# Preparing the mixture's first expert and four tiles inside the cross attention, widening four tiles at a time, and counting the first stage's loads apart

## The chip, the cores and the metric

The kernel runs on one core of a Trainium2 chip. The core has five engines that matter here, each with its own queue of instructions, carried out in order: TensorE (PE in the profile, PEld for its weight loads), VectorE (DVE), ScalarE (ACT), GpSimd (POOL) and SyncE (SP), which here only issues transfers between HBM and the on-chip memory SBUF. Matmuls write into eight PSUM banks of 128 partitions by 512 fp32 values. Engines wait for each other through counting semaphores. The metric is the time of the whole program on the device in microseconds (us), the median of three runs.

## The reference

Two decoder layers over 32 sequences of 64 rows with 256 features, so 2048 rows, 16 tiles of 128 rows. Each of the six sublayers takes a layer norm of x and adds its result to x:

```python
x = x + _L0_attn_ref(_layernorm(x), ...)                      # differential attention with rotary, causal
x = x + _L0_xattn_ref(_layernorm(x), ctx_2048, ctx_2048, W)   # attention over features
x = x + _L0_ffn_ref(_layernorm(x), ...)
x = x + _L1_attn_ref(_layernorm(x), ...)                      # state space
x = x + _L1_xattn_ref(_layernorm(x), ctx_2048, mask, ...)     # grouped cross attention, 16 heads of 128
x = x + _L1_ffn_ref(_layernorm(x), ...)                       # mixture of 8 experts
```

The mixture is what most of the change is about (Wg, Wu, Wd are 8 x 256 x 256):

```python
weights = _router_weights(x, Wr, temperature)
gate = jnp.einsum('btd,edf->ebtf', x, Wg)
up = jnp.einsum('btd,edf->ebtf', x, Wu)
...
mid = jax.nn.silu(gate) * up
out = jnp.einsum('ebtf,efd->ebtd', mid, Wd)
...
return jnp.einsum('bte,ebtd->btd', weights, out)
```

Two of the eight experts have a low-rank addition to each matrix.

## The kernel before

The six sublayers follow one another; at each end all semaphores are cleared and all engines meet at a barrier (`end_sublayer`, L59 to L63). x stays in SBUF throughout. A layer norm (`RowNorm`) has three parts: small DVE steps on the row statistics (`on_vector`), two ACT steps (`on_scalar`), and one DVE operation for each tile (`normalise`, L119). `keep_clock` (L74 to L77) issues matmuls of the identity whose result nobody reads; each shows as two PE rows of the trace.

**Stage one, `differential_attention`.** A hand-written software pipeline: `turn(t)` for t from -3 to 16, in which tile t+3 is normalised, turned (a transpose through PE) and projected, tile t+2 is rotated by the rotary tables, tile t+1 is scored and tile t is mixed. The order of each engine is the order in which `turn` is written. SP loads x in four parts of 512 KB, the identity, the projections and seven constants; the seven share one semaphore, `loaded`, with LOADS = 7 * 16. At the end of its turn -3 DVE runs `lambda_dots`, which waits for all seven; DVE's next steps are the second tile's normalisation and the first rotation. PE waits for the same semaphore, and for `wo_scaled`, before it projects the second tile.

**The cross attention, `grouped_attention`.** Again turns; LAST is 15, the turn of the last tile, and turn 16 mixes that tile, multiplies it with the output weights (L2386, L2390) and adds it to x (L2266). The sublayer owns three large buffers shared with the one before: `raw` (called `staged` by the caller), `w_q_high` and `w_q_low`. The last queries read the two halves of w_q in turn 14.

**Split operands.** For fp32 accuracy at the speed of the fp32r type a number is kept as a high part (an ACT or DVE cast) and a low part (the number less its high part). `three_passes` (L1919 to L1923) is three matmuls: high by high, low by high, high by low. Every large matmul of the cross attention and of the mixture goes through L1923 or is written out in the same way.

**The mixture, `mixture`.** x is taken as PAIRS = 8 pairs of tiles, and there are STEPS = 64 steps, step s being expert s // 8 and pair s % 8. On PE a step is widen(s), then a few small jobs in the first steps (turn_x, route_x, fold), then narrow(s - 2):

- widen(s): for each half f of the 256 middle features, gate and up, each over two chunks of 128 inputs in three passes. That is 12 matmuls of 256 columns for each f, 24 in a step. The results of one f lie in one bank, gate in its first half and up in its second.
- then ACT takes silu of the gate (L2589), DVE multiplies with up (`middle`, L2723), ACT casts the product to its high part (`middle_high`, L2576), DVE subtracts to get the low part (`middle_low`, L2728).
- narrow(s): 12 matmuls of 256 columns with the down matrix. It waits until both low parts of step s are there. DVE adds the result to x, weighted by the router (`add`, L2748; for expert one also `add_held`, L2734).

Before the first widening the mixture loads expert 2's three matrices (M_ORDER starts with 2), casts and subtracts them, and normalises, turns and splits the first pair. PE fills this time with `keep_clock`.

## Time and profile before

| | us |
|---|---|
| three runs, median (lowest to highest) | 1317.61 (1316.46 to 1317.67) |
| the profiled execution, its own time | 1319.73 |
| its span, first to last instruction | 1317.8 |
| PE busy | 1205.5 (91% of the span) |
| DVE busy | 961.0 (73%) |
| ACT busy | 707.0 (54%) |
| POOL busy | 464.9 (35%) |
| mean granted PE clock | 0.974 of full speed |

Full speed of the PE clock is 2.4 GHz, and it is granted in two levels, 2.4 and 1.2 GHz; in a window row the clock is a mean over the window. A bracket at the end of a timeline row gives how long the engine sat idle before it and what released it. The duration of a matmul row reaches to its modelled end, past the start of the next one, so PE's pace is read from the distance of starts.

### The profile page before, as it was taken

What the parts mean: (1) busy time and instruction counts of PE and PEld (TensorE: products, weight loads), DVE (VectorE), ACT (ScalarE), POOL (GpSimd) and SP (SyncE); (2) the same over time, 40 slices, a digit from 0 to 9 for tenths busy, and PEclk for the clock granted to TensorE, in tenths of its full rate; (3) what the DMA queues carried; (4) which work ended last, traced back from release to release, by engine and by line L of the source; (5) the groups of instructions that cost most, each with busy time, mean ns of one, the idle gap of its engine ahead of it and who ended that gap; (6) DMA issues with size and microseconds to landing.
All of it is one profiled execution on the core that took longest, in us unless ns stands there. A gap on an engine that the chain in (4) does not pass through costs nothing. (4 is left out here: it accounts for less than half of the span.)

```text
span 1317.8 us, 27466 instructions
## 1 busy us (share of the span) xinstructions
PE 1205.5 (91%) x9944; PEld 958.4 (73%) x9944; DVE 961.0 (73%) x1862; ACT 707.0 (54%) x1459; POOL 464.9 (35%) x553
## 2 busy tenths in 40 slices
PE   4999997988888778898899999999997999999998
PEld 3677764444443657797678878787886999999998
DVE  5889986899996467786668777786775768555555
ACT  2778863788888355001565665656562563333332
POOL 1444642456563134565552324233230301112210
PEclk8999997899999879899999999999999999999999
DMA  5111161133331300001200000000000300000001
GB/s 174 37 36 37 43 150 34 42 81 96 90 88 30 114 1 0 1 0 65 85 9 4 8 4 4 8 4 8 4 1 11 87 25 25 25 25 25 1 1 65
DMA packets 60709, 51.05 MB, mean 39 GB/s; under 512 B 9064, under 2 KB 52936, under 8 KB 60232
## 3 DMA queue, kind: packets, MB, share of 16 engines
q1 hardware_dynamic: 60622, 49.88, 13.6%
q8 instruction: 56, 0.92, 0.3%
q14 instruction: 31, 0.25, 0.1%
HBM read 37.93 MB, written 11.53 MB: 38 GB/s over the span
## 5 line engine op out<-in xcount | busy, mean ns | idle before, releaser
L208 DVE TENSOR_REDUCE stacks_neg_max<-psum 128x2 f32<-128x512 f32 x256 | 164.0, 686 | 29.1 <-PE psum L204 28.1
L947 ACT ACTIVATE fa_probs<-psum 128x1024 f32<-128x1024 f32 x128 | 130.7, 1023 | 36.0 <-PE psum L1072 36.0
L1923 PE MATMUL psum<-mo_xT_high,mo_w_high 128*128 128x256 f32 x512 | 144.5, 282 | 1.7 <-DVE mo_xT_low L2757 1.6
L1923 PE MATMUL psum<-mo_xT_low,mo_w_high 128*128 128x256 f32 x512 | 144.2, 282 | 0.0
L1923 PE MATMUL psum<-mo_xT_high,mo_w_low 128*128 128x256 f32 x512 | 143.5, 280 | 0.0
L2589 ACT ACTIVATE mo_silu<-psum 128x256 f32<-128x256 f32 x128 | 49.0, 384 | 155.0 <-PE psum L1923 155.0
L2723 DVE TENSOR_TENSOR mo_mid<-mo_silu,psum 128x256 f32<-128x256 f32 x128 | 53.6, 420 | 92.8 <-ACT mo_silu L2589 92.7
L2059 POOL TENSOR_TENSOR ga_probs<-ga_probs,ga_top 128x1024 f32<-128x1024 f32 x16 | 30.5, 1904 | 203.7 <-DVE ga_top L2213 203.7
L204 PE MATMUL psum<-stacks_k_stack,stacks_q_stack 48*128 48x256 bf16 x512 | 89.8, 283 | 9.9 <-DVE stacks_neg_max L208 6.5
L1923 PEld LDWEIGHTS psum<-mo_xT_high,mo_w_high 128*128 128x128 f32 x512 | 96.3, 188 | 2.2 <-DVE mo_xT_low L2757 1.7
L1923 PEld LDWEIGHTS psum<-mo_xT_low,mo_w_high 128*128 128x128 f32 x512 | 96.4, 188 | 0.0
L1923 PEld LDWEIGHTS psum<-mo_xT_high,mo_w_low 128*128 128x128 f32 x512 | 96.3, 188 | 0.0
L2530 POOL TENSOR_TENSOR mo_w_low<-mo_raw,mo_w_high 128x512 fp32r<-128x512 f32 x21 | 27.6, 1314 | 188.0 <-ACT mo_w_high L2564 188.0
L1072 PE MATMUL psum<-stacks_q_stack,stacks_k_stack 51*128 51x256 bf16 x512 | 86.8, 280 | 0.0
L2048 POOL TENSOR_TENSOR ga_q_scaled<-ga_q,ga_q_inv 128x1024 f32<-128x1024 f32 x32 | 70.1, 2191 | 38.0 <-ACT ga_q_inv L2090 38.0
L204 PEld LDWEIGHTS psum<-stacks_k_stack,stacks_q_stack 48*128 48x128 bf16 x512 | 32.7, 96 | 64.2 <-DVE stacks_neg_max L208 36.4
L2083 ACT ACTIVATE ga_q_scaled<-ga_q 128x512 f32<-128x512 f32 x64 | 40.2, 632 | 61.8 <-DVE ga_q L2186 61.8
L1923 PE MATMUL psum<-mo_w_high,mo_mid_high 128*128 128x256 f32 x256 | 72.3, 282 | 0.0
L1923 PE MATMUL psum<-mo_w_low,mo_mid_high 128*128 128x256 f32 x256 | 71.9, 281 | 0.0
L1923 PE MATMUL psum<-mo_w_high,mo_mid_low 128*128 128x256 f32 x256 | 71.7, 280 | 0.0
L1084 PE MATMUL psum<-fa_probs,fa_values 128*32 128x256 f32 x1024 | 70.3, 393 | 0.8 <-ACT fa_probs L947 0.6
L2386 PE MATMUL psum<-ga_w_o_high,ga_mixedT_high 128*128 128x256 f32 x256 | 64.2, 291 | 4.9 <-DVE ga_mixedT_low L2205 4.9
(432 smaller groups left out, 3548.3 us busy)
## 6 DMA issues: line engine op xcount, KB each, us to landing
k_parts<-da_k_parts SPq DMA_DIRECT2D x96, 64.0 KB, 2.0
stacks_k_stack<-k_parts SPq DMA_DIRECT2D x32, 192.0 KB
q_parts<-stacks_parts SPq DMA_DIRECT2D x48, 64.0 KB, 2.0
stacks_q_stack<-q_parts SPq DMA_DIRECT2D x32, 96.0 KB
x<-in_x SPq DMA_DIRECT2D x4, 512.0 KB, 7.7
da_context<-in_ctx SPq DMA_DIRECT2D x4, 512.0 KB, 7.3
stacks_q_stack<-q_parts SPq DMA_DIRECT2D x32, 64.0 KB
fa_context<-in_ctxT SPq DMA_DIRECT2D x16, 128.0 KB, 2.3
```

The costliest lines, as they stand in the source:

```text
L204: return core.nc.tensor.matmul(core.psum[:, bank, q * E:(q + 1) * E], self.q_stack[lane, slot, b, h // LANES, q * P:(q + 1) * P], self.k_s ...
L208: return core.nc.vector.tensor_reduce(self.neg_max[:, b, :, head_at(h)], core.psum[:, bank, :].rearrange("p (q k) -> p q k", q=2), AX.X, A ...
L947: nc.scalar.activation(probs[:, g].rearrange("p h k q -> p h (k q)"), ps[:, 2 + 2 * (g % 2):4 + 2 * (g % 2), :], ACT.Exp).then_inc(exp_don ...
L1072: return nc.tensor.matmul(ps[:, 2 + h % 4, k * E:(k + 1) * E], k_stack[lane, slot, b, h // LANES, k * P:(k + 1) * P], q_stack[lane, slot, ...
L1084: done = nc.tensor.matmul(ps[32 * c:32 * c + 32, 6, half * E:(half + 1) * E], values[:, slot, k, 8 * b + head_at(h), :], probs[:, h // 2, ...
L1923: done = nc.tensor.matmul(out, lhsT[i], rhs[j], start=start and k == 0, stop=stop and k == 2)
L2048: nc.gpsimd.tensor_tensor(q_scaled[:, columns].rearrange("p (h d) -> p h d", d=G_HD), q[:, columns].rearrange("p (h d) -> p h d", d=G_HD), ...
L2059: nc.gpsimd.tensor_tensor(probs[:], probs[:], top[:, :, None].to_broadcast([P, G_HEADS, SEQ]), ALU.subtract).then_inc(shifted, 1)
L2083: nc.scalar.activation(q_scaled[:, g * G_CHUNK:(g + 1) * G_CHUNK], q[:, g * G_CHUNK:(g + 1) * G_CHUNK], ACT.Square).then_inc(squares_ready, 1)
L2386: nc.tensor.matmul(ps[:, 6, 0:E], mixedT_high[:, h], weight[:, h], start=(h == 0 and weight is w_o_high), stop=False)
L2589: nc.scalar.activation(silu[:, j % 4], ps[:, j % 4, 0:2 * P], ACT.Silu).then_inc(silu_ready, 1)
L2723: nc.vector.tensor_tensor(mid[:, j % 4], silu[:, j % 4], ps[:, j % 4, 2 * P:4 * P], ALU.mult).then_inc(mid_ready, 1)
```

## The change

It has three parts.

1. In stage one the loads are reordered and counted in three groups: `rotary_loaded` (rotary tables and head mask), `causal_loaded`, and `loaded` with three loads left. The identity comes first, x in part 1 comes behind the rotary tables, parts 2 and 3 later still. `lambda_dots` moves from DVE's turn -3 to its turn -2. PE runs `keep_clock(core, 6, 12)` before the pipeline and `keep_clock(core, 6, 8)` in turn -1.
2. The cross attention's last two turns prepare the mixture. SP loads the first expert's matrices into `staged`; in turn 15 ACT casts them and POOL subtracts them (into the space of w_q_high and w_q_low), and DVE normalises eight tiles with a layer norm of its own for these (`lead_ln`); in turn 16 PE turns the first four tiles, ACT copies them, DVE casts them and POOL subtracts them. The mixture uses these buffers in place of its own and starts with widen(0).
3. The mixture widens four tiles at once: widen(s) is now one half f for two pairs, 12 matmuls of 512 columns, gate in one bank and up in another. silu, middle, middle_high and middle_low run once a step on 512 columns in place of twice on 256. narrow(s) waits for the low parts of both steps of its four tiles, and the last four narrowings follow the last widening.

```diff
@@ differential_attention
+        loaded, rotary_loaded, causal_loaded = sem("loaded"), sem("rotary_loaded"), sem("causal_loaded")
-        LOADS = 7 * 16
+        LOADS = 3 * 16
...
+            first_rows.load_ident(sp)
             first_rows.load(sp, 0)
-            first_rows.load_ident(sp)
-            for out, src in ((w_qk[:], chunked(dram["da_w_qk"])), (w_v[:], chunked(dram["da_w_v"]))):
+            for out, src in ((w_v[:], chunked(dram["da_w_v"])), (w_qk[:], chunked(dram["da_w_qk"]))):
                 sp.dma_start(out, src).then_inc(projection_loaded, 16)
-            for g in range(1, first_rows.PARTS):
-                first_rows.load(sp, g)
-            for out, src in ((rotary[:], dram["rotary"]),
-                             (head_mask[:], dram["da_head_mask"]), (causal[:], dram["causal"]), (causal_rows[:], dram["causal_rows"]),
-                             (lam_in[:], dram["da_lam"]), (w_o[:], chunked(dram["da_w_o"])), (gain[:], dram["da_gain"]),
-                             ):
+            for out, src in ((rotary[:], dram["rotary"]), (head_mask[:], dram["da_head_mask"])):
+                sp.dma_start(out, src).then_inc(rotary_loaded, 16)
+            first_rows.load(sp, 1)
+            for out, src in ((causal[:], dram["causal"]), (causal_rows[:], dram["causal_rows"])):
+                sp.dma_start(out, src).then_inc(causal_loaded, 16)
+            first_rows.load(sp, 2)
+            for out, src in ((lam_in[:], dram["da_lam"]), (w_o[:], chunked(dram["da_w_o"])), (gain[:], dram["da_gain"])):
                 sp.dma_start(out, src).then_inc(loaded, 16)
+            first_rows.load(sp, 3)
...
@@ vector engine
+                    if at(t, -2):
+                        dve.wait_ge(rotary_loaded, 32)
...
-                if isinstance(t, int) and t == -3:
+                if isinstance(t, int) and t == -2:
                     lambda_dots()
...
@@ tensor engine
+                    if at(t, -1):
+                        pe.wait_ge(causal_loaded, 32)
+                    if at(t, 0):
+                        pe.wait_ge(wo_scaled, KC)
...
+                if at(t, -1):
+                    keep_clock(core, 6, 8)
...
-                    if at(t, -2):
-                        pe.wait_ge(loaded, LOADS)
-                        pe.wait_ge(wo_scaled, KC)
...
+            keep_clock(core, 6, 12)
             pipeline(pe, turn)
@@ grouped_attention, sync
+            for k, name in enumerate(("gate", "up", "down")):
+                sp.dma_start(ahead.raw[:, k], chunked(dram[f"mo_w_{name}"][M_ORDER[0]])).then_inc(ahead_loaded, 16)
...
@@ gpsimd engine
+                if isinstance(t, int) and t == LAST:
+                    for k in range(M_MATRICES):
+                        pool.wait_ge(ahead_w_highs, k + 1)
+                        nc.gpsimd.tensor_tensor(ahead.w_low[:, k], ahead.raw[:, k], ahead.w_high[:, k].bitcast(F32), ALU.subtract).then_inc(ahead_w_lows, 1)
+                if isinstance(t, int) and t == TILES:
+                    for n in range(ahead.PAIRS):
...
+                        nc.gpsimd.tensor_tensor(ahead.pair(ahead.xT_low, n), ahead.xT[:, n], ahead.pair(ahead.xT_high, n).bitcast(F32),
...
@@ scalar engine
+                if isinstance(t, int) and t == LAST:
+                    act.wait_ge(ahead_loaded, 16 * M_MATRICES)
+                    act.wait_ge(q_psum, 4 * TILES)
+                    for k in range(M_MATRICES):
+                        nc.scalar.copy(ahead.w_high[:, k], ahead.raw[:, k]).then_inc(ahead_w_highs, 1)
+                if isinstance(t, int) and t == TILES:
+                    for n in range(ahead.PAIRS):
+                        act.wait_ge(ahead_xT_psum, n + 1)
+                        nc.scalar.copy(ahead.xT[:, n].rearrange("p c t -> p (c t)"), ps[:, 2 + n, :]).then_inc(ahead_xT_ready, 1)
...
@@ vector engine
+                if isinstance(t, int) and t == LAST:
+                    dve.wait_ge(lead_ln.ready, 1)
...
+                    for n in range(ahead.TILES):
+                        lead_ln.normalise(ahead.xn[:, n // 2, n % 2], n).then_inc(ahead_xn, 1)
+                if isinstance(t, int) and t == TILES:
+                    for n in range(ahead.PAIRS):
...
+                        nc.vector.tensor_copy(ahead.pair(ahead.xT_high, n), ps[:, 2 + n, :].rearrange("p (c t) -> p c t", c=KC)).then_inc(ahead_x_highs, 1)
...
@@ tensor engine
-                        keep_clock(core, 2, 8)
+                        keep_clock(core, 2, 4)
                     pe.wait_ge(v_lows, t)
+                    if isinstance(t, int) and t == TILES:
+                        for n in range(ahead.PAIRS):
+                            turn_ahead(n)
@@ mixture, scalar
-                for f in range(FT):
-                    j = FT * s + f
-                    act.wait_ge(wide_psum, j + 1)
-                    nc.scalar.activation(silu[:, j % 4], ps[:, j % 4, 0:2 * P], ACT.Silu).then_inc(silu_ready, 1)
-                    if j >= 1:
-                        middle_high(j - 1)
+                act.wait_ge(wide_psum, s + 1)
+                nc.scalar.activation(silu[:, s % 2], ps[:, s % 2 * 2 + GATE, :], ACT.Silu).then_inc(silu_ready, 1)
+                middle_high(s)
...
@@ vector engine
-                if s >= PAIRS + LAG + 1:
+                if PAIRS + LAG + 1 <= s < STEPS - 1:
                     add(s - LAG - 1)
...
+                middle(s)
+                middle_low(s)
...
@@ tensor engine
             def widen(s):
+                e, q, f = s // PAIRS, s % PAIRS // 2, s % 2
+                for k in (GATE, UP):
+                    for c in range(KC):
+                        columns = slice(f * P, (f + 1) * P)
+                        done = three_passes(nc, ps[:, s % 2 * 2 + k, :],
+                                            (w_high[e % RING][:, k, c, columns], w_low[e % RING][:, k, c, columns]),
+                                            (xT_high[q][:, c], xT_low[q][:, c]), start=(c == 0), stop=(c == KC - 1))
+                done.then_inc(wide_psum, 1)
...
+                pe.wait_ge(mid_ready, s - 1)
+                widen(s)
...
-                pe.wait_ge(mid_lows, FT * (s + 1))
+                pe.wait_ge(mid_lows, s // 2 * 2 + 2)
...
-            keep_clock(core, 2, 5)
-            turn_x(0)
-            keep_clock(core, 2, 4)
+            pe.sem_inc(xT_psum, ahead.PAIRS)
...
-                if s >= LAG:
+                if LAG <= s < STEPS - 2:
                     narrow(s - LAG)
-            for s in range(STEPS - LAG, STEPS):
+            for s in range(STEPS - LAG - 2, STEPS):
                 narrow(s)
```

DVE in stage one, from the first tile's normalisation (da_xn) on. Before:

```order
L119 TENSOR_SCALAR da_xn<-x,da_lead_mean,da_lead_rstd 128x256
L148 BN_STATS row_stats<-x 128x6 x4
L517 TENSOR_TENSOR da_lam_prod<-da_lam_in 128x16
L519 TENSOR_REDUCE da_lam_dot<-da_lam_prod 128x2
L521 TENSOR_SCALAR da_w_o<-da_w_o,da_gain 128x256 x2
L119 TENSOR_SCALAR da_xn<-x,da_lead_mean,da_lead_rstd 128x256
L559 TENSOR_TENSOR da_rot_b<-psum,da_rotary 128x384
```

And DVE after the change, in the same place:

```order
L119 TENSOR_SCALAR da_xn<-x,da_lead_mean,da_lead_rstd 128x256
L148 BN_STATS row_stats<-x 128x6 x4
L119 TENSOR_SCALAR da_xn<-x,da_lead_mean,da_lead_rstd 128x256
L567 TENSOR_TENSOR da_rot_b<-psum,da_rotary 128x384
L568 TENSOR_TENSOR da_rot_a<-psum,da_rotary 128x384
L574 STREAM_SHUFFLE da_rot_c<-da_rot_b 128x384
L590 TENSOR_TENSOR da_rot<-da_rot_a,da_rot_c 128x384
L148 BN_STATS row_stats<-x 128x6 x4
L523 TENSOR_TENSOR da_lam_prod<-da_lam_in 128x16
```

The lambda steps have moved behind the second tile's normalisation, its rotation and the third part's statistics.

PE from the end of the cross attention into the mixture, before (the two branches stand at the barrier, mo_xn are the normalised rows of the first pair):

```order
L2390 MATMUL psum<-ga_w_o_high,ga_mixedT_low 128x256 x16
L77 MATMUL psum<-ident 128x128 x4
L1938 UNCONDITIONAL_BRANCH
L2784 UNCONDITIONAL_BRANCH
L77 MATMUL psum<-ident 128x128 x5
L2793 MATMUL psum<-ident,mo_xn 128x128 x4
L77 MATMUL psum<-ident 128x128 x4
L1923 MATMUL psum<-mo_xT_high,mo_w_high 128x256
```

And PE after the change; here w_q_high and w_q_low hold the first expert and the first four tiles:

```order
L2455 MATMUL psum<-ga_w_o_high,ga_mixedT_low 128x256 x16
L77 MATMUL psum<-ident 128x128 x4
L1950 UNCONDITIONAL_BRANCH
L2851 UNCONDITIONAL_BRANCH
L1935 MATMUL psum<-w_q_high 128x512
L1935 MATMUL psum<-w_q_high,w_q_low 128x512
L1935 MATMUL psum<-w_q_low,w_q_high 128x512
```

Nothing stands between the barrier and the first widening, and that has 512 columns.

DVE in the cross attention's turn 15 and the start of turn 16, after the change (staged is where the eight normalised tiles go; before, the row with x8 at L119 and the row at L2314 are not there):

```order
L2304 TENSOR_TENSOR ga_probs<-ga_probs,ga_inv 128x1024
L119 TENSOR_SCALAR staged<-x,ga_lead_mean,ga_lead_rstd 128x256 x8
L2317 TENSOR_TENSOR x<-x,psum 128x256
L2326 TENSOR_TENSOR ga_probsT_low<-psum,ga_probsT_high 128x1024
L2330 BN_STATS row_stats<-x 128x6
L2246 SCALAR_TENSOR_TENSOR ga_mixedT_low<-psum,ga_bias_v,ga_mixedT_high 128x4x64 x8
L2314 CAST w_q_high<-psum 128x2x256 x2
```

The eight normalisations stand ahead of tile 14's addition to x, and the two casts ahead of tile 15's.

## Rows read from the trace of the kernel before

**Rows 1.** The chain that ended last: start us, us, what, in the mixture.

```profile
1066.74 246.87 PE psum L1923 x2088
```

**Rows 2.** Timeline, stage one: start us, us, engine, line, operation, [idle before <-releaser].

```profile
10.00 1.41 DVE L148 BATCH_NORM_STATS2 row_stats<-x 128x6 f32<-128x256 f32 x4 [1.69 <-DMA x<-in_x]
...
15.48 0.18 DVE L517 TENSOR_TENSOR da_lam_prod<-da_lam_in 128x16 f32<-128x16 f32 x1 [4.08 <-DMA da_gain<-in_da_gain]
...
16.30 0.41 DVE L119 TENSOR_SCALAR da_xn<-x,da_lead_mean,da_lead_rstd 128x256 f32<-128x256 f32 x1
...
18.93 2.77 PE L762 MATMUL psum<-da_xT,da_w_qk 128*128 128x128 f32 x12
18.96 1.90 POOL L408 TENSOR_TENSOR da_keys<-da_rot,da_head_mask 128x1024 f32<-128x1024 f32 x1 [16.54 <-DVE da_rot L582]
...
21.63 0.61 PE L653 MATMUL psum<-da_causal,da_causal_rows 64*128 64x512 bf16 x2
...
23.69 1.23 DVE L537 TENSOR_REDUCE da_top<-psum 128x16 f32<-128x1024 f32 x1 [0.86 <-PE psum L657]
...
28.81 1.50 PE L762 MATMUL psum<-da_xT,da_w_qk 128*128 128x128 f32 x12
```

**Rows 3.** Windows: stretch, length, busy time by engine, granted clock, DMA share, GB/s.

```profile
4.00:8.00 4.00, 0.00 (x0) 0.00 (x0) 2.23 (x13) 0.50 (x2) 0.00 (x0) 1.00 0.99 338
16.00:20.00 4.00, 2.77 (x12) 2.37 (x12) 3.90 (x12) 1.27 (x6) 1.04 (x1) 0.50 0.84 261
```

**Rows 4.** Timeline, the cross attention's last two turns, columns as in rows 2.

```profile
999.70 1.23 DVE L2263 TENSOR_TENSOR ga_probs<-ga_probs,ga_inv 128x1024 f32<-128x1024 f32 x1
...
1004.28 1.01 ACT L2169 CAST ga_probsT_high<-psum 128x1024 fp32r<-128x1024 f32 x1 [6.69 <-PE psum L2415]
...
1016.67 0.42 DVE L2266 TENSOR_TENSOR x<-x,psum 128x256 f32<-128x256 f32 x1 [4.48 <-PE psum L2390]
```

**Rows 5.** Timeline, the mixture's start, PE and ACT, then DVE and POOL behind.

```profile
1018.90 1.35 PE L77 MATMUL psum<-ident 128*128 128x128 f32 x10 [1.38 <-PEq L62]
...
1021.60 0.62 ACT L2564 CAST mo_w_high<-mo_raw 128x512 fp32r<-128x512 f32 x1 [1.20 <-DMA mo_raw<-in_mo_w_gate]
...
1024.33 0.39 PE L1923 MATMUL psum<-mo_xT_high,mo_w_high 128*128 128x256 f32 x1 [1.55 <-DVE mo_xT_low L2757]
...
1026.04 1.38 DVE L119 TENSOR_SCALAR mo_xn<-x,mo_mean,mo_rstd 128x256 f32<-128x256 f32 x4
...
1031.62 2.57 POOL L2518 TENSOR_TENSOR mo_xT_low<-mo_xT,mo_xT_high 128x512 fp32r<-128x512 f32 x2 [0.96 <-DVE mo_xT_high L2630]
...
1032.06 2.93 DVE L119 TENSOR_SCALAR mo_xn<-x,mo_mean,mo_rstd 128x256 f32<-128x256 f32 x4
```

**Rows 6.** Timeline, PE's pace: 512 columns in the cross attention, 256 in the mixture.

```profile
856.34 0.39 PE L1923 MATMUL psum<-w_q_high,ga_xT_low 128*128 128x512 f32 x1
...
857.26 0.39 PE L1923 MATMUL psum<-w_q_low,ga_xT_high 128*128 128x512 f32 x1
...
857.69 0.69 DVE L2186 TENSOR_TENSOR ga_q<-psum,ga_bias_q 128x512 f32<-128x512 f32 x1 [0.55 <-PE psum L1923]
...
873.06 0.41 PE L1923 MATMUL psum<-ga_w_k_high,ga_ctxT_low 128*128 128x512 f32 x1
...
874.00 0.39 PE L1923 MATMUL psum<-ga_w_k_low,ga_ctxT_high 128*128 128x512 f32 x1
...
1102.19 0.28 PE L1923 MATMUL psum<-mo_xT_high,mo_w_high 128*128 128x256 f32 x1
...
1105.04 0.28 PE L1923 MATMUL psum<-mo_w_high,mo_mid_high 128*128 128x256 f32 x1
```

**Rows 7.** Timeline, mixture: a steady step's first two links, and a loaded step's DVE.

```profile
1089.31 1.92 DVE L2734 SCALAR_TENSOR_TENSOR x<-mo_held,mo_zone,x 128x256 f32<-128x256 f32 x2
...
1197.39 0.38 ACT L2589 ACTIVATE mo_silu<-psum 128x256 f32<-128x256 f32 x1 [1.64 <-PE psum L1923]
...
1197.80 0.42 DVE L2723 TENSOR_TENSOR mo_mid<-mo_silu,psum 128x256 f32<-128x256 f32 x1 [0.96 <-ACT mo_silu L2589]
```

219 lines of the change are left out of this document (115 added, 104 removed).

## The prediction, made before the changed kernel ran

> **What bounds the kernel now.** I read the chain of waits first, to see which engine ends last at each of the three places of the change, then the timelines there. In the mixture the chain stays on PE: its last piece is 2088 matmuls in 246.87 us, 0.1182 us each [rows 1]. So there PE's pace is the bound, and ACT, DVE and POOL cost nothing as long as they deliver in time. Between the barrier and 1024.33 it is not PE's pace that decides: PE issues clock-keeping matmuls from 1018.90 and waits for the first split operands [rows 5]. In stage one DVE is what the others follow: it idles 4.08 us for the seventh small load (da_gain), and at 16.30 makes the rows on which PE's second projection rests [rows 2]. The last turns of the cross attention are gaps on every engine but PE [rows 4].
>
> **Stage one.** DVE's order today: statistics of x's part 1 at 10.00 for 1.41, then the wait to 15.48, then the second normalisation at 16.30 [rows 2]. Afterwards no lambda wait stands between the two. Part 1 of x, however, now comes behind the rotary tables (384 KB). At 338 GB/s [rows 3] that is 1.15 us, so it lands near 11.1 in place of 10.0; the statistics end near 12.5 and the second normalisation starts there: 3.8 us earlier. The identity now goes ahead of x's part 0, one more issue of 0.5 us, which delays only the first tile and ends before DVE needs it.
>
> PE follows. Twelve rows of the projection take 2.77 us at 18.93, but 1.50 at 28.81 [rows 2]. The granted clock of 16 to 20 is 0.50 [rows 3], the level of 1.2 GHz; 1.50 is what the level of 2.4 GHz gives. PE had done nothing before its first turn, and idled before 16.77. The change fills the time from the identity's landing (near 3) to the first turn with 12 clock-keeping matmuls. I take it that the clock is then at its upper level for the second turn. Then the second tile goes so: normalised 12.9, turned 13.4, copied 14.0, projected with v (0.6) and q, k (1.5) by 16.3. The first keys come after rot_b, rot_a, shuffle and sum (together 2.2 us) and POOL's 1.90 [rows 2]: 12.9 + 2.2 + 1.9 = 17.0. The first scores start at 17.2 in place of 21.63 and take about 0.3 less, so the first maximum starts near 19.0 in place of 23.69 [rows 2]. DVE itself is free by then: rotation to 15.1, statistics of part 2 to 16.5, lambda steps 0.8 to 17.3, normalisation and two rotations to 18.7. From 23.69 on nothing changes in order but 8 clock-keeping matmuls, 16 PE rows or 2.0 us, where PE waits 2 us for DVE anyway. The gain is 4.6 us. If the clock stays at 1.2 GHz, PE decides: the second projection ends near 19.0 and the gain is 2.2. With part 1 landing as early as before it is at most 5.4.
>
> **The cross attention's last turns.** All that is added must fit into gaps; I price it engine by engine. ACT: three casts of 128x512 at 0.62 [rows 5] lie in its gap of 6.69 before 1004.28 [rows 4], two copies of 0.58 behind the last mixed heads. POOL: three subtractions of 128x512, 1.3 each [rows 5], between about 998.3 and 1002.5, and two in turn 16 that end near 1015.5, 2 us ahead of DVE's last operation; it has nothing else there. PE: 4 clock-keeping matmuls give way to 8 transposes, 8 rows for 8 rows. SP: three transfers, with nothing queued behind them but waits. DVE: eight normalisations start when the probabilities are done at 1000.93 [rows 4]. Four take 1.38 us alone, but 2.93 beside POOL's two subtractions [rows 5]: about 0.8 us extra for each subtraction overlapped. Here some 1.5 us of POOL are overlapped, so they take 2.8 + 1.0 = 3.8 and end near 1004.9. Queued behind them are tile 14's addition (0.42, as at 1016.67) and the low part of the probabilities, which cannot start before ACT ends at 1005.29 [rows 4]. That leaves 0.1 us of loss; with all eight slowed they take 5.9, and the loss would be 2.1. The two casts in turn 16 lie in DVE's gap of 4.48 before 1016.67 [rows 4].
>
> **The mixture's start.** PE could start at 1018.90, the first thing it does after the barrier, and starts real work at 1024.33 [rows 5]. Gain 5.4 us. What is late next? widen(0) and widen(1) need nothing more. widen(2) needs the second four tiles: their transposes follow widen(0) and end at 1018.9 + 2.8 + 1.0 = 1022.7; copies, casts and two subtractions of 1.3 bring them to about 1026.5, and PE comes to widen(2) at 1029.7. The four transposes of pair 1 are gone from PE's path too, 0.5 us at the pace of the keeping rows (ten in 1.35) [rows 5]. Together 5.9 us (5.4 to 5.9).
>
> **The widening.** 1536 matmuls of 256 columns become 768 of 512. From 1102.19 to 1105.04 are 24 starts, 0.1187 each, 0.2375 for two. In the cross attention four distances of 512-column matmuls take 0.92 us at 856.34 and 0.94 us at 873.06, so 0.230 and 0.235 each [rows 6]. The difference to 0.2375, times 768, is 5.8 us by the one and 1.9 by the other, and these are the bounds. Neither place is nearer to the mixture than the other, so I take the middle, 0.2325: 768 x 0.005 = 3.8 us.
>
> The Trainium skill, page TensorE: Matmul & The Clock Gate, section Back-to-back issue gap, puts the isolated gap at N/2.4 + 2.5 ns. By it, an estimate, two short matmuls cost 2.5 ns more than one long one and the 768 pairs save 1.9 us, the lower bound again. The 256-column rows lie 12 ns above N/2.4, so the trace doesn't agree with the fixed part.
>
> **The new wait.** narrow(s) for even s now waits for the low parts of widen(s+1). Between the end of widen(s+1) and that narrow PE has narrow(s-1) (12 x 0.118 = 1.4) and widen(s+2) (12 x 0.2325 = 2.8): 4.2 us of cover, where there were 8.5. The chain it must cover: hand-over from PE 0.2 (DVE starts at 857.69, 0.43 after the last 512-column start) [rows 6], silu 0.62, product 0.69, cast 0.62, subtraction 0.69 [rows 5, 6], three hand-overs of 0.03 [rows 7]: 2.9, say 3.0. It holds in steady steps. Two places are tighter. In the last steps narrow(62) has only narrow(60) and narrow(61) as cover, 2.8 us: a loss of 0.2. In the second expert's steps DVE has add_held beside POOL's subtraction, 1.92 us for two [rows 7] where two additions like that at 1016.67 would take 0.84 [rows 4]; three such steps in a row push the products back by about 1.1 us each, against 1.2 us of slack, which I follow through the queue to a loss of 0.4. Together 0.6 (0.2 to 3).
>
> **The sum.** 4.6 - 0.1 + 5.9 + 3.8 - 0.6 = 13.6 us. The profiled execution would come out at 1319.73 - 13.6 = 1306.1; it lies 2.1 above the median of the runs, so the forecast for the median is 1317.6 - 13.6 = 1304.0.
>
> **Rivals.**
> - The clock does not hold in stage one. For: PE's work there has gaps, and the trace shows the fall after such a gap. Against: the gaps are shorter now. Gain 2.2 in place of 4.6, so 1306.4.
> - The long matmuls keep a pace of 0.235 [rows 6]: 1.9 less 3.8 is 1.9 us lost, 1305.9.
> - The preparation is late or in the way: the eight normalisations hold back turn 15 by 2.1 us in place of 0.1: 1306.0. For: DVE and POOL slow each other [rows 5]. Against: only 1.5 us of POOL's work is left by then.
> - By the Trainium skill (the same page, Part 4: PE-mode transpose) a transpose does not keep the clock up as a matmul does. As a mechanism here: PE's eight clock-keeping rows give way to transposes at 1005, the clock falls to 1.2 GHz, and the 48 output matmuls run slower until it rises. Priced from the projection's 2.77 against 1.50 us for twelve rows, a stretch of 3 us at the lower level loses 1.4 us, so 1305.4, or twice that, 1306.8, if it lasts into widen(0). Against it: 8 matmul rows and all of the mixing stand beside the transposes in the same stretch.
> - Slower: the cover of 4.2 us does not hold in steady steps. The place is narrow(s) for 31 even s; the price is what the chain has above 4.2. It turns the change slower when 31 times the excess passes 13.6 us, that is from 0.44 us, a chain of 4.64. At 5.0 the excess is 0.8, and 31 x 0.8 = 25 us less 13.6 gives 1329. Against: the sum of rows is 3.0, and it needs a slowdown of ACT or DVE that no steady row shows.
> - The change doesn't do what it says, because the barrier and not the preparation sets the mixture's start: then 5.4 shrinks to 1 or 2, giving 1308. Against: clock-keeping matmuls start at 1018.90 already.
>
> **Chances.** Forecast 0.50; clock in stage one 0.20; pace 0.10; preparation late or transposes 0.13; steady waits slower 0.03; barrier 0.04. The range reaches from all upper bounds at once, 5.4 + 5.9 + 5.8 less 0.3, that is 1317.6 - 16.8 = 1300.8 and a little more, to two rivals together with the new wait at its bound, 1310: 1299.5 to 1309.5. About 0.2% or 2.6 us is what a measurement can tell from no change. All cases but the steady waits lie more than 7 us below: faster 0.95, same 0.02, slower 0.03.
>
> **What would show it.** The first widening row right behind the barrier, where the clock-keeping row stands today; no PE gap of over 0.5 us in the mixture but near steps 12 to 14 and narrow(62); starts of 512-column matmuls 0.2325 apart; the first maximum of stage one near 19.0 and its projection of the second tile in 1.5 us. A PE idle row ended by mo_mid_low in every second step would make the forecast wrong, as would a lambda or x wait of DVE past 13 us in stage one, or a cross-attention turn 15 longer than before.

## The result, and the profile after

The changed kernel takes 1305.56 us, the median of five runs (1303.46 to 1310.16); the kernel before takes 1317.61 (1316.46 to 1318.76) beside it. The ratio is 0.9914, with a 95% interval of 0.9898 to 0.9931, that is 9.1 to 13.4 us. Measured once more, the distance of the medians was 13.5 us (1305.40 against 1318.95, ratio 0.9914, 0.9891 to 0.9936). The forecast was 1304.0 with a range of 1299.5 to 1309.5. The ratios leave out one execution of the kernel before that took 2291.62 us.

The profiled execution of after took 1305.56 us, 14.2 less than that of before. Its page begins:

```profile
span 1303.5 us, 25721 instructions
PE 1201.9 (92%) x9190; PEld 920.7 (71%) x9190; DVE 946.5 (73%) x1737; ACT 697.7 (54%) x1333; POOL 470.2 (36%) x557
```

PE's busy time falls by only 3.6 us (1205.5 to 1201.9); the rest of the 14 us was waiting. These are the three places of the change.

**Stage one.** Timeline of after, DVE, PE and ACT (start us, us, engine, line, operation, [idle before <-releaser]); the rows answer to [rows 2]:

```profile
9.93 1.41 DVE L148 BATCH_NORM_STATS2 row_stats<-x 128x6 f32<-128x256 f32 x4 [0.81 <-DMA x<-in_x]
11.38 0.41 DVE L119 TENSOR_SCALAR da_xn<-x,da_lead_mean,da_lead_rstd 128x256 f32<-128x256 f32 x1
12.96 0.56 DVE L567 TENSOR_TENSOR da_rot_b<-psum,da_rotary 128x384 f32<-128x384 f32 x1 [1.18 <-PE psum L773]
...
19.15 1.21 DVE L543 TENSOR_REDUCE da_top<-psum 128x16 f32<-128x1024 f32 x1
```

```profile
10.63 2.23 PE L773 MATMUL psum<-da_xT,da_w_qk 128*128 128x128 f32 x12
...
14.70 1.50 PE L773 MATMUL psum<-da_xT,da_w_qk 128*128 128x128 f32 x12
...
17.32 0.39 PE L661 MATMUL psum<-da_causal,da_causal_rows 64*128 64x512 bf16 x2 [1.12 <-POOL da_keys L414]
```

The lambda wait is gone and the first maximum starts at 19.15 in place of 23.69, 4.54 us earlier. The second normalisation comes at 11.38, 4.9 us earlier. But DVE then waits 1.18 us for the first tile's projection, and the granted clock shows why. Windows of after (stretch, length, busy time by engine, granted clock, DMA share, GB/s):

```profile
8.00:11.00 3.00, 1.41 (x11) 1.12 (x11) 1.48 (x6) 1.05 (x4) 0.00 (x0) 1.00 1.12 343
11.00:14.00 3.00, 2.54 (x14) 2.14 (x13) 1.78 (x7) 1.24 (x5) 0.00 (x0) 0.53 1.11 336
14.00:17.00 3.00, 2.20 (x16) 2.01 (x16) 2.86 (x7) 1.04 (x4) 1.68 (x1) 0.90 1.09 385
```

The fall to 1.2 GHz has not gone. It stands at 11 to 14, on the first projection; the second, which lay in it before ([rows 3], 2.77), now runs in 1.50. The first was slow before as well, which neither the rows above nor the granted clock told. Timeline of before, PE:

```profile
10.59 2.44 PE L762 MATMUL psum<-da_xT,da_w_qk 128*128 128x128 f32 x12
```

The first maximum isn't the end of the stage. From it to the moment when PE passes the barrier behind stage one are 191.42 us before and 192.32 after, so of the 4.54 us 3.64 are left there (215.11 against 211.47). The prediction had put nothing for this loss of 0.9. The two sequences of maxima part by 0.28 at the fourth maximum and by 0.9 at the twentieth.

**The cross attention's last turns.** Timeline of after, PE, DVE and ACT; then the same two PE rows of before:

```profile
990.29 0.39 PE L2451 MATMUL psum<-ga_w_o_high,ga_mixedT_high 128*128 128x256 f32 x1 [2.53 <-DVE ga_mixedT_low L2246]
...
995.85 3.63 DVE L119 TENSOR_SCALAR staged<-x,ga_lead_mean,ga_lead_rstd 128x256 f32<-128x256 f32 x8
998.67 1.01 ACT L2210 CAST ga_probsT_high<-psum 128x1024 fp32r<-128x1024 f32 x1 [5.38 <-PE psum L2480]
999.73 1.21 DVE L2326 TENSOR_TENSOR ga_probsT_low<-psum,ga_probsT_high 128x1024 fp32r<-128x1024 f32 x1
1001.00 0.39 PE L2365 MATMUL psum<-ga_probsT_high,ga_values_high 64*128 64x256 f32 x2 [0.60 <-DVE ga_probsT_low L2326]
```

```profile
996.15 0.58 PE L2386 MATMUL psum<-ga_w_o_high,ga_mixedT_high 128*128 128x256 f32 x1 [2.53 <-DVE ga_mixedT_low L2205]
...
1006.65 0.38 PE L2303 MATMUL psum<-ga_probsT_high,ga_values_high 64*128 64x256 f32 x2 [0.62 <-issue]
```

From the first output matmul to the first mixing matmul it is 10.71 us now and was 10.50, but 10.77 in a second profile of before. DVE begins the low part at 999.73, 0.05 after ACT has ended (998.67 + 1.01 = 999.68). So two things end together here, and one profile can't say which is the limit; no_keep, below, can.

**The mixture's start.** Timeline of after; the row answers to those at 1018.90 and 1024.33 in [rows 5]:

```profile
1013.46 0.47 PE L1935 MATMUL psum<-w_q_high 128*128 128x512 f32 x1 [1.60 <-PEq L62]
```

The mixture's chain begins at 1013.27 and widening starts 0.19 later; before it was 1018.79 and 5.54. That is 5.35 us.

**The steps.** I count a step from the start of one widening to the next. Steps 0 to 9 take 55.74 us after (1013.46 to 1069.20) and 56.60 before; steps 10 to 61 take 218.65 after (1069.20 to 1287.85) and 221.17 before. From there to the end it is 15.7 in both. The chain of waits of after, in the mixture (start us, us, what), shows the one long interruption:

```profile
1054.77 1.63 PE psum L1935 x12
1056.39 0.02 issue
1056.42 0.59 ACT mo_held L2659
1057.00 0.02 issue
1057.02 1.28 ACT L2691
...
1062.72 0.70 DVE mo_mid_low L2804
1063.42 0.04 issue
1063.46 230.14 PE psum L1935 x1308
```

ACT loads its table for the router's exponentials (1.28), DVE's router steps follow, and the middle values of step 7 queue behind them. PE waits only 0.23 us for it: widening 8 takes 3.03 from its start to the next narrowing in place of 2.80.

In the pair of profiles, then, read from barrier to barrier: stage one 3.64; the second sublayer 0.72 and the third 0.30, which the change doesn't touch; the cross attention 0.94, in spite of 1.4 won in its first turn, which the change doesn't touch either; the mixture 8.66, of which 5.35 are its start, 0.86 steps 0 to 9 and 2.52 steps 10 to 61. That is 14.2 us, of which some 2 lie where no gain was forecast.

### The profile page after: what moved, and what is told of

The parts are those of the page before. It is cut to its first block and busy times, and to the rows that moved or that the text cites. A ratio compares the mean times of both kernels' runs of the same rounds, so it can differ in the third digit from the quotient of the medians.

```text
span 1303.5 us, 25721 instructions
## 1 busy us (share of the span) xinstructions
PE 1201.9 (92%) x9190; PEld 920.7 (71%) x9190; DVE 946.5 (73%) x1737; ACT 697.7 (54%) x1333; POOL 470.2 (36%) x557
## 5 line engine op out<-in xcount | busy, mean ns | idle before, releaser
L2672 ACT ACTIVATE mo_silu<-psum 128x512 f32<-128x512 f32 x64 | 38.3, 598 | 113.2 <-PE psum L1935 113.1
L2800 DVE TENSOR_TENSOR mo_mid<-mo_silu,psum 128x512 f32<-128x512 f32 x64 | 43.9, 685 | 73.0 <-ACT mo_silu L2672 72.9
L2804 DVE TENSOR_TENSOR mo_mid_low<-mo_mid,mo_mid_high 128x512 fp32r<-128x512 f32 x64 | 44.9, 702 | 44.0 <-ACT mo_mid_high L2663 44.0
L2663 ACT CAST mo_mid_high<-mo_mid 128x512 fp32r<-128x512 f32 x64 | 39.7, 620 | 56.4 <-DVE mo_mid L2800 56.4
L2451 PE MATMUL psum<-ga_w_o_low,ga_mixedT_high 128*128 128x256 f32 x256 | 62.9, 286 | 0.0
L2246 DVE SCALAR_TENSOR_TENSOR ga_mixedT_low<-psum,ga_bias_v,ga_mixedT_high 128x256 fp32r<-128x256 f32 x128 | 52.9, 476 | 8.6 <-ACT ga_mixedT_high L2124 8.6
L1935 PE MATMUL psum<-w_q_high,ga_xT_high 128*128 128x512 f32 x128 | 54.9, 429 | 3.5 <-DVE ga_q L2227 1.2
L1401 POOL TENSOR_TENSOR fs_inputs<-fs_xn_kept,fs_decay_dt 128x1536 f32 (+1 forms) x16 | 47.7, 2982 | 27.1 <-PE psum L1898 21.4
L2451 PEld LDWEIGHTS psum<-ga_w_o_high,ga_mixedT_high 128*128 128x128 f32 x256 | 49.3, 193 | 11.3 <-issue 5.6
L2227 DVE TENSOR_TENSOR ga_q<-psum,ga_bias_q 128x512 f32<-128x512 f32 x64 | 43.6, 683 | 12.2 <-PE psum L1935 8.9
```

What stands on the lines that cost most here:

```text
L1401: nc.gpsimd.tensor_tensor(inputs[:, place(2)].rearrange("p m (h d) -> p m h d", d=S_HD), by_head(xn_kept[:, t + 2, :])[:, None].to_broadca ...
L1935: done = nc.tensor.matmul(out, lhsT[i], rhs[j], start=start and k == 0, stop=stop and k == 2)
L2246: done = nc.vector.scalar_tensor_tensor(low, mixed_of(j)[:, b], bias_v[:, j:j + 1], high.bitcast(F32), ALU.add, ALU.subtract)
L2451: nc.tensor.matmul(ps[:, 6, 0:E], mixedT_high[:, h], weight[:, h], start=(h == 0 and weight is w_o_high), stop=False)
L2800: nc.vector.tensor_tensor(mid[:, j % 4], silu[:, j % 2], ps[:, j % 2 * 2 + UP, :], ALU.mult).then_inc(mid_ready, 1)
L2804: nc.vector.tensor_tensor(of_middle(mid_low, j), mid[:, j % 4], of_middle(mid_high, j).bitcast(F32), ALU.subtract).then_inc(mid_lows, 1)
```

## The experiments

All times are medians; ratios are to the kernel before, measured beside each: 1318.95 for after_again, stage_undone, split_256 and own_slot, 1317.91 for before_again, no_keep, x_first and route_spread, 1318.54 for the rest. "First max" is the start of da_top in stage one, "stage" the time at which PE passes the barrier behind it, "third" the time from the third widening's start to the next PE job; these and the last two columns are from one profile each.

| kernel | us | ratio (95%) | first max | stage | third | steps 0-9 | steps 10-61 |
|---|---|---|---|---|---|---|---|
| before | 1317.61 | 1 | 23.69 | 215.11 | 2.93 | 56.60 | 221.17 |
| before_again | 1321.32 (one run) | | 22.58 | 214.32 | 2.94 | 56.61 | 221.17 |
| after | 1305.56 | 0.9914 (0.9898-0.9931) | 19.15 | 211.47 | 2.88 | 55.74 | 218.65 |
| after_again | 1305.40 | 0.9914 (0.9891-0.9936) | 18.12 | 210.46 | 4.43 | 57.26 | 218.65 |
| stage_undone | 1309.94 | 0.9931 (0.9918-0.9944) | 21.33 | 212.78 | 4.44 | 56.96 | 218.64 |
| split_256 | 1310.01 | 0.9932 (0.9912-0.9951) | 19.43 | 211.50 | 4.27 | 57.81 | 221.83 |
| own_slot | 1305.57 | 0.9899 (0.9880-0.9917) | 19.21 | 211.44 | 4.21 | 57.31 | 218.02 |
| no_keep | 1308.93 | 0.9933 (0.9913-0.9953) | 20.11 | 212.30 | 2.90 | 55.71 | 218.63 |
| x_first | 1305.77 | 0.9913 (0.9892-0.9934) | 19.66 | 211.93 | 4.43 | 57.23 | 218.64 |
| route_spread | 1307.06 | 0.9915 (0.9889-0.9940) | 19.74 | 212.11 | 2.88 | 58.93 | 218.64 |
| route_even | 1306.29 | 0.9905 (0.9890-0.9921) | 19.13 | 211.54 | 2.88 | 55.47 | 220.39 |
| combined | 1304.60 | 0.9900 (0.9882-0.9919) | 20.09 | 214.05 | 2.88 | 55.45 | 219.81 |
| chain_2 | 1313.38 (one run) | | 19.30 | 211.70 | 4.22 | 58.32 | 219.29 |
| chain_3 | 1325.76 (one run) | | 19.46 | 211.89 | 4.11 | 61.45 | 227.32 |

**Both kernels once more.** Nothing in them changed.

> The changed kernel once more, to tell what of its distance to the kernel before is the change and what is the one profiled execution. In the first pair of profiles the cross attention's first turn (from its first transpose to the sum over the scaled queries) was 1.4 us shorter after the change, though the change does not touch it. If that is scatter of transfers (the bias of q landed later in one of the two), this profile shows the distance from the barrier's first transpose to ga_q_sum anywhere between 8.3 and 9.8 us, and the median lies at 1305.5 +- 1.5. If the change causes it, the distance is 8.3 again. The pace of the 512-column matmuls shows its pattern by expert (0.231 and 0.234 us) again if it comes from where the operands lie, another pattern if it is scatter.

> The kernel before, one more profiled execution, for two readings that rested on one trace. First, the clock in stage one: in the first profile before it was at 1.2 GHz for 6.8 us from 16.0 on, in stage_undone (the same stage one) for 3.4 us, and the first maximum stood at 23.69 and at 21.33. Theory: the stage of before has both lengths by chance, so the first maximum is at 21.3 or 23.7 here. Second, the mixture's start: if the clock falls to 1.2 GHz in the third widening only after the change (it did in four of five profiles of kernels with the new mixture), all widenings behind the start are 2.84 to 2.96 us here; if it is chance in both kernels, one may be 4.3.

The pace by expert came back to the hundredth (218.65 twice), so it is no scatter. Other sublayers scatter by much more: the cross attention takes 400.4 and 402.7 in the two profiles before and 399.5 to 404.0 in those of changed kernels. The first turn of the cross attention, from its first transpose to ga_q_sum, took 9.74 and 9.58 in the two profiles before, 8.33 and 8.70 in the two after, and 8.2 to 8.9 in nine others of changed kernels, but 9.93 in no_keep; the waits in it end on transfers. I can't tell whether the change has a part in that; the tables don't count it. The first maximum before came at 22.58, between the two values expected, so the theory of two lengths is not borne out.

New is the third widening: 4.43 us in after_again. Timeline of it, PE:

```profile
1018.27 1.85 PE L2871 MATMUL psum<-mo_w_route,ahead_xT 128*128 128x8 f32 x16
1019.97 1.93 PE L2871 MATMUL psum<-mo_w_route,mo_xT 128*128 128x8 f32 x16
1021.76 1.07 PE L2860 MATMUL psum<-ident,staged 128*128 128x128 f32 x8
1022.59 0.48 PE L1935 MATMUL psum<-mo_xT_high,w_q_high 128*128 128x512 f32 x1
...
1023.66 0.63 PE L1935 MATMUL psum<-mo_xT_high,w_q_high 128*128 128x512 f32 x1
1024.09 0.63 PE L1935 MATMUL psum<-mo_xT_high,w_q_low 128*128 128x512 f32 x1
```

And its window, the clock being the third number from the end:

```profile
1023.00:1027.00 4.00, 4.00 (x12) 3.15 (x11) 3.88 (x6) 0.51 (x2) 2.56 (x2) 0.57 0.00 0
```

The starts at 1023.66 and 1024.09 are 0.43 us apart, 512 columns at 1.2 GHz. It costs 1.5 us (57.26 against 55.74). Neither profile of before has it; seven of the nine kernels whose router stands as in the change do, all but after and no_keep.

**The first stage as before.**

```diff
-        LOADS = 3 * 16
+        LOADS = 7 * 16
...
-                if isinstance(t, int) and t == -2:
+                if isinstance(t, int) and t == -3:
                     lambda_dots()
...
-            keep_clock(core, 6, 12)
             pipeline(pe, turn)
```

> The changed kernel with the first stage as it was before (loads, semaphore, lambda step, no clock-keeping). Theory, the prediction's first term: 4.5 us are lost again, so about 4.5 us above after_again in the same call, and the first maximum stands near 23.7 in place of 19.15. Rival: part of the stage's gain is given back before the end of the stage (in the first pair of profiles the distance shrank from 4.5 to 3.9 us by 238), then the whole costs 3.9. If the gain were only the clock, nothing of the order: 2.4.

By the medians 4.5 us are lost, by the ratios 0.17% or 2.2 us, with intervals that overlap. The first maximum came at 21.33. It is the lambda wait's end that scatters: the three profiles with the old stage have 23.69, 22.58 and 21.33, on average 22.5; nine with the new stage, x_first and no_keep aside, have 18.12 to 20.09, on average 19.3. That is 3.2 us at the first maximum. But the way from there to the barrier took 191.4 to 191.7 us in the three and 192.1 to 192.4 in eight of the nine (193.96 in combined), so about 0.8 us is given back. At the barrier the averages are 214.07 and 211.80: the stage is worth some 2.3 us. What gives the 0.8 back isn't shown; the clock-keeping doesn't, for no_keep has 192.2 as well.

The 4.5 us of the medians agree with the forecast by luck. The two profiled executions, 1309.94 and 1305.47, lie at the medians, and between them stage one ends 2.32 later, the second sublayer is 1.56 longer, the third 2.86 shorter, the cross attention 3.84 longer and the mixture 0.32 shorter. One thing there may be more than scatter: the second sublayer took 227.3 to 227.7 us in the three profiles with the old stage one, and 224.4 to 227.4, on average 225.7, in the eleven with the new. No run tests it.

**Without the clock-keeping.**

```diff
-                if at(t, -1):
-                    keep_clock(core, 6, 8)
...
-            keep_clock(core, 6, 12)
```

> The changed kernel without the clock-keeping matmuls in stage one (12 ahead of the pipeline, 8 in turn -1). The prediction put 2.4 us on them: without them the second tile's projection would take 2.8 us in place of 1.5 and the first maximum would stand 2.4 us later than with them. Profiles with them have it at 18.12 (clock never low) and at 19.15 to 19.43. Theory of the prediction: 21.5 here, the clock at 1.2 GHz somewhere between 10 and 20, and the time 2.4 us above after_again. Rival: the clock falls anyway for 3.4 us in either, and DVE hides it; then the first maximum is at 19 to 20 and the time 0 to 1 us above.

Timeline of no_keep, PE:

```profile
11.04 2.77 PE L771 MATMUL psum<-da_xT,da_w_qk 128*128 128x128 f32 x12
...
15.34 1.50 PE L771 MATMUL psum<-da_xT,da_w_qk 128*128 128x128 f32 x12
```

The second projection runs at full speed without any clock-keeping. Only the first is slow, and in after it is nearly as slow (2.23). Over all profiles the second projection takes 2.20 to 2.77 in the three with the old stage, where PE idled 1.8 to 3.7 us just before that tile, and 1.50 to 1.56 in all eleven with the new one, where it idled 1.3 at most. So the full speed goes with the order of loads and waits, which draws PE's work together. The clock-keeping helps the first projection, and not always: it took 1.50 in three of the ten profiles that have it and 2.23 to 2.77 in the other seven, 2.44 to 2.77 in the four that don't. The first maximum of no_keep is at 20.11, 0.8 behind the average with clock-keeping, and the stage ends 0.5 behind (212.30 against 211.80). Both lie near the edge of the scatter (combined, with clock-keeping, has 20.09 and 214.05), so by these figures the clock-keeping is worth about 1 us or less, perhaps nothing, and not 2.4. The median of no_keep is 3.5 us above that of after_again; by the two profiled executions 1.8 of that is stage one and 2.9 the cross attention. Its ratio's interval begins at 0.9913, and after's ratio is 0.9914.

This profile also shows what sets the pace of the last turns. In it PE's clock did not fall during the output matmuls of tile 14. Timeline of no_keep, ACT and DVE, then its windows:

```profile
999.05 1.01 ACT L2207 CAST ga_probsT_high<-psum 128x1024 fp32r<-128x1024 f32 x1 [3.88 <-PE psum L2477]
1001.30 0.41 DVE L2314 TENSOR_TENSOR x<-x,psum 128x256 f32<-128x256 f32 x1
1001.64 1.21 DVE L2323 TENSOR_TENSOR ga_probsT_low<-psum,ga_probsT_high 128x1024 fp32r<-128x1024 f32 x1
```

```profile
1005.00:1008.00 3.00, 1.07 (x9) 1.07 (x10) 2.78 (x8) 2.31 (x5) 0.00 (x0) 1.00 0.00 0
1008.00:1011.00 3.00, 3.00 (x18) 3.00 (x17) 1.64 (x4) 0.00 (x0) 1.88 (x2) 0.53 0.00 0
```

ACT is ready at 1000.06 and DVE begins the low part only at 1001.64: here the added work holds it back by 1.6 us. Counted from the first output matmul, the low part begins 9.44 to 9.48 behind in eleven of the twelve profiles of changed kernels (9.31 in combined), whether ACT is ready at 7.89 or at 9.45. So DVE is the limit now; before, the low part began 9.18 and 9.44 behind, right after ACT. And from 1008.2 to 1011.6 the clock is at 1.2 GHz, over output matmuls of tile 15: from the first mixing matmul to the barrier it takes 13.79 us, where the others take 12.2 to 12.3.

**x's first part ahead of the identity.**

```diff
-            first_rows.load_ident(sp)
             first_rows.load(sp, 0)
+            first_rows.load_ident(sp)
```

> The changed kernel with the two first issues of SP changed about: part 0 of x ahead of the identity. In the profile of after part 0 starts DVE at 5.77 (before the change 4.95), the first projection ends near 12.9, and DVE idles 1.18 us for it at 12.96 before the first rotation. Theory: the order of the two issues costs 0.8 us on the path, so the first maximum comes at 18.3 to 18.6 in place of 19.15 to 19.4, and 0.8 us are won. Rival: the keys on POOL and the second tile's turn set the pace, nothing won. If the clock-keeping starts later with the identity and does not hold the clock, up to 2.4 us are lost.

Nothing won: x came at 4.71 in place of 5.77, but the identity only at 4.92 in place of 2.69, and PE, which must first work through its 12 clock-keeping matmuls, turned the first tile at 10.21 in place of 9.18. The clock stayed up (both projections 1.50), the maximum stood at 19.66. The rival is half borne out: the first scores waited 1.63 us for POOL's keys. What came ahead of the keys was the first tile and not the second, for DVE waited 2.09 us for PE's first projection.

**256 columns again.**

```diff
-                    for c in range(KC):
-                        columns = slice(f * P, (f + 1) * P)
-                        done = three_passes(nc, ps[:, s % 2 * 2 + k, :],
...
+                    for half in range(2):
+                        part = slice(half * 2 * P, (half + 1) * 2 * P)
+                        for c in range(KC):
+                            columns = slice(f * P, (f + 1) * P)
+                            done = three_passes(nc, ps[:, s % 2 * 2 + k, part],
```

> The changed kernel, each 512-column matmul of the mixture's widening issued as two of 256 columns into the halves of the same bank; all else, also the four-tile steps and waits, is as after the change. It takes the pace apart from the rest of part three. The steady steps of the two profiles differ by 2.5 us over 52 steps, 0.0485 a step, so 3.1 us over 64. Theory: this kernel is 3.1 us slower than after_again, a widening of 24 matmuls takes 2.84 to 2.85 us in every expert. Rival (the prediction's term): 3.8 us. Rival: no difference, if the steps' pace were set by the four-tile chain.

Steps 10 to 61 take 221.83, 3.18 us more than after, so the whole gain of the steady steps, and a little more, is the pace of the long matmuls. It is also 0.66 more than before took with 256 columns: here too some experts have another pace (2.87 for a widening in steps 18 to 23, 2.80 in 24 and 25, 2.84 to 2.85 in 26 to 31), where before had 2.84 everywhere.

**A third buffer for the weights.**

```diff
-        w_high, w_low = ((first_half, sb(name, [P, MATRICES, KC, M_FF], F32R))
+        w_high, w_low = ((first_half, sb(name, [P, MATRICES, KC, M_FF], F32R), sb(name + "2", [P, MATRICES, KC, M_FF], F32R))
...
+        def slot(e):
+            return 2 if e and e % 2 == 0 else e % 2
```

> The changed kernel, but experts at positions 2, 4 and 6 keep their split matrices in a third buffer of the mixture's own in place of the space of w_q_high and w_q_low. In the profile of after a widening takes 2.77 to 2.78 us where its weights and its rows lie in the same region (both in w_q's space, or both in the mixture's own), and 2.81 to 2.82 where the weights lie in w_q's space and the rows in the mixture's own (steps 18 to 23, 34 to 39, 50 to 55). Theory, the place decides: these steps fall to 2.77 to 2.78, and 18 steps x 0.035 = 0.6 us are won, 0.8 at most. Rival, something else goes with every second expert (buffer number, the transfer of the next one): the steps stay at 2.81 and nothing is won.

Widening 20 (start to start of the narrowing behind it) in after, then in own_slot:

```profile
1111.16 0.40 PE L1935 MATMUL psum<-mo_xT_high,w_q_high 128*128 128x512 f32 x1
...
1113.97 0.28 PE L1935 MATMUL psum<-w_q_high,mo_mid_high 128*128 128x256 f32 x1
```

```profile
1115.15 0.39 PE L1935 MATMUL psum<-mo_xT_high,mo_w_high 128*128 128x512 f32 x1
...
1117.93 0.28 PE L1935 MATMUL psum<-mo_w_high,mo_mid_high 128*128 128x256 f32 x1
```

That is 2.81 and 2.78. All eighteen steps fell to 2.77 or 2.78, and the six of steps 16, 17, 32, 33, 48 and 49, whose rows lie in w_q's space and whose weights now don't, rose from 2.78 to 2.80. The theory of the place holds on both sides. The gain is 0.63 us in steps 10 to 61, as expected; the medians can't show it.

**The router's matmuls spread.** In route_spread pairs 2 and 3 go behind widening 2, 4 to 7 behind widening 3. In route_even two pairs go behind each of widenings 1 to 4, and the logits, the low-rank products and the routing come a step later.

```diff
-                if s == 1:
-                    route_x(0)
-                    route_x(1)
-                if 1 <= s < 4:
-                    route_x(2 * s)
-                    route_x(2 * s + 1)
+                if 1 <= s < 5:
+                    route_x(2 * s - 2)
+                    route_x(2 * s - 1)
...
-                if 4 <= s < 10:
-                    route(s - 4)
+                if 5 <= s < 11:
+                    route(s - 5)
```

> The changed kernel, with the router's matmuls spread otherwise: pairs 0 and 1 behind widening 1, 2 and 3 behind widening 2, 4 to 7 behind widening 3, in place of 0 to 3 behind widening 1, 4 and 5 behind 2, 6 and 7 behind 3. In the changed kernel 32 router matmuls of 8 columns and 8 transposes stand in a row for 4.3 us, and in four of five profiles the clock is at 1.2 GHz for 3.4 us from the following widening on, which takes 4.2 to 4.4 us in place of 2.85. Theory: the row of small matmuls causes it; spread, no widening of the start is over 3.0 us, and 1.5 us are won in the median, most scatter above aside. Rival: the fall is of the place (so many us behind the barrier) or moves behind the new row of 32 at widening 3; then the same 1.5 us are lost in widening 2 to 4.

> The changed kernel with the router's matmuls two pairs at a time behind widenings 1, 2, 3 and 4 (32 was the longest row in a piece so far, 16 now), and the logits, the low-rank products and the steps of the routing one step later each. Theory: rows of small matmuls of over 4 us bring the clock down behind them (32 of 8 columns and 8 transposes behind widening 1 did in five of seven profiles; with 32 behind widening 3 the fall moved there, and no such row, as in both profiles before, no fall). With rows of 2.6 us at most no widening of the start takes over 3.0 us; the mixture's first ten steps take 55.7 us in place of 57.3 and the median lies 1.5 us below the changed kernel's, near 1304. Rival: the fall is of the place; then it comes anyway.

> route_even and own_slot together: the even router and the third buffer. Theory: 1.5 + 0.6 = 2.1 us below the changed kernel, near 1303.3; steps 10 to 62 take 218.0 us and the first ten 55.7. Rival: the scatter of 1 to 2 us that clock and transfers bring hides it in the time, and only the trace shows it.

In route_spread the third widening is well (2.88), and the fall sits with the new row of 32: it begins in its second half, which takes 2.87 in place of 1.93, and lasts 6.8 us, over the narrowing and into widening 4. Steps 0 to 9 take 58.93. Its windows:

```profile
1032.00:1036.00 4.00, 4.00 (x30) 4.00 (x29) 1.38 (x2) 0.94 (x2) 0.00 (x0) 0.75 0.01 2
1036.00:1040.00 4.00, 4.00 (x17) 3.71 (x18) 0.00 (x0) 1.36 (x3) 0.00 (x0) 0.50 0.00 0
```

In route_even and combined no widening of the first ten is over 2.91, and these steps take 55.47 and 55.45. So the row of small matmuls brings the fall, not the place: it followed the row when the row moved, and was absent in the two kernels without such a row, as in the two profiles of before. That is one profile each, and the fall also stays away in two of the nine with the row in its place, so this is likely and not certain. But the gain was given back. Steps 10 to 61 take 220.39 in route_even, 1.74 more, in two waits that after doesn't have. The first of them:

```profile
1080.22 0.39 PE L1935 MATMUL psum<-mo_w_high,mo_mid_high 128*128 128x256 f32 x1 [0.63 <-DVE mo_mid_low L2804]
```

The routing, one step later, now meets the additions of the second expert on DVE. All in all route_even stands where after stands (1306.29, ratio 0.9905). combined has the lowest median of all, 1304.60, with the ratio 0.9900 (0.9882 to 0.9919); it can't be told from the changed kernel.

**The chain made longer.** ACT copies the gate's bank two or three times before silu; nobody reads the copies.

```diff
                 act.wait_ge(wide_psum, s + 1)
+                if s:
+                    act.wait_ge(spared, 3 * s)
+                for n in range(3):
+                    nc.scalar.copy(spare[:, n], ps[:, s % 2 * 2 + GATE, :]).then_inc(spared, 1)
```

> The changed kernel with work added that nobody reads: in each step of the mixture ACT copies the gate's bank twice (128x512, 0.6 us each) before it takes silu. It lengthens the chain from the end of widening s+1 to its low part, which is 2.9 us in the profile of after (silu 0.60, product 0.69, cast 0.62, subtraction 0.69, hand-overs), to 4.1 us. The cover is narrow(s-1) and widening s+2, 1.41 + 2.81 = 4.2 us. Theory, the prediction's: no PE wait in steady steps; only the last narrowings come 1.2 us later, and the first steps where ACT has most to do may lose 1 to 2 us. So 1.2 to 3.5 us above after_again by its span. Rival: slack is used up elsewhere (additions ahead of the product on DVE), then each of 31 pairs of steps loses up to 1.2 us, 37 us.

> The same with three copies: the chain is 4.7 us against a cover of 4.2. Theory: every second narrowing (even s) waits 0.5 us, 31 x 0.5 = 15 us, and 1.8 at the end, so 15 to 20 us above after_again: slower than the kernel before. This is the slower rival of the prediction made real, which was to decide from a chain of 4.64 us on. Rival: ACT's copies are hidden by later steps, nothing lost; or ACT itself becomes the bound.

From its first widening to its end chain_2 takes 294.3 us, after_again 291.6: 2.7 more, within what was expected. Steady steps don't wait; widening 8 does (4.08) and widening 14 (3.37), the steps in which routing and additions load DVE. chain_3 takes 307.9, 16.3 more, and is slower than before: 4.2 of it in steps 0 to 9, where a stretch of 3.4 us at 1.2 GHz that the others don't have (from 1070.6) is in the sum, 8.7 in steps 10 to 61 and 3.4 behind them. Steady steps of chain_3, ACT, DVE and PE:

```profile
1137.66 1.56 ACT L2676 COPY mo_spare<-psum 128x512 f32<-128x512 f32 x3 [1.07 <-PE psum L1935]
1139.10 0.63 ACT L2677 ACTIVATE mo_silu<-psum 128x512 f32<-128x512 f32 x1
```

```profile
1139.75 0.69 DVE L2805 TENSOR_TENSOR mo_mid<-mo_silu,psum 128x512 f32<-128x512 f32 x1 [1.66 <-ACT mo_silu L2677]
1141.13 0.69 DVE L2809 TENSOR_TENSOR mo_mid_low<-mo_mid,mo_mid_high 128x512 fp32r<-128x512 f32 x1 [0.69 <-ACT mo_mid_high L2664]
```

```profile
1137.46 0.28 PE L1935 MATMUL psum<-w_q_high,mo_mid_high 128*128 128x256 f32 x1
...
1141.44 0.39 PE L1935 MATMUL psum<-w_q_low,mo_w_high 128*128 128x512 f32 x1
1141.88 0.39 PE L1935 MATMUL psum<-w_q_high,mo_mid_high 128*128 128x256 f32 x1
```

Widening 23 ended at 1137.46; its low part is there at 1141.82, a chain of 4.36, since a copy in a row of three costs 0.48 and not 0.6. Narrowing comes 4.42 behind, where 1.41 + 2.81 = 4.22 is free. With the slow start behind a wait (the narrowing takes 1.52 in place of 1.41) each pair of steps loses 0.33 us: 8.67 us over the 26 pairs of steps 10 to 61.

## Why the prediction was right, and where not

The forecast of 13.6 us stands against 12.0 and 13.5 by the medians and 11.3 by both ratios. Its mechanisms hold; the sizes came out differently, and that the sum is so near is partly luck. For the mixture 9.1 were forecast (5.9 + 3.8 - 0.6): its length fell from 298.9 to 290.25 in after and 291.80 in after_again, so 8.7 and 7.1. For stage one 4.6 were forecast, and 2.3 are there on average. What fills the gap in the profiles lies in sublayers for which no gain was forecast: 2.0 us in the first pair (the second sublayer 0.72, the third 0.30, the cross attention 0.94), 4.8 between before_again and after_again.

- **Stage one, 4.6 forecast.** At the first maximum 4.54 in the pair of profiles and some 3.2 over all; at the barrier 3.64 and some 2.3. "From 23.69 on nothing changes in order" put nothing for the rest of the stage, which is about 0.8 longer. Before the maximum two steps were wrong and cancelled. Part 1 of x was to land at 11.1 behind the rotary tables; it landed at 9.93 in after (9.4 to 11.3 in the eleven profiles with the new stage), and the second normalisation came at 11.38, not 12.5. But the clock fell on the first projection, DVE waited for that, and the first scores waited for POOL's keys at 17.32. "I take it that the clock is then at its upper level for the second turn" was right as to the second projection (1.50); the reason was wrong, since no_keep has it too. That rival, 2.4 us for the clock, named the right term and mis-sized it: from after_again, where both projections took 1.50, to after, where the first took 2.23, the first maximum moves by 1.03.
- **The base.** The old stage's end of the lambda wait scatters by over 2 us (21.33 to 23.69 for the first maximum), and the one profile I reckoned from was the latest of three. This is the term most in need of a range, and its range in the prediction came from other causes.
- **The last turns, 0.1 forecast.** From the first output matmul to the mixing it is 10.58 to 10.76 in the twelve profiles of changed kernels, against 10.51 and 10.77 before: between 0.3 and nothing. The working was off in one step. POOL's subtractions begin where I had them (992.32, 2.03 behind the first output matmul, 2.15 forecast), but they also lie beside DVE's product of the probabilities, which takes 2.08 in place of 1.23. So the normalisations start 0.8 later than forecast; they take 3.63 (3.8 forecast). That this costs so little is due to the clock: in all profiles but no_keep a stretch at 1.2 GHz during tile 14's output matmuls makes ACT late too. In no_keep, where it is missing, the added work costs the 1.6 us that would have been won.
- **The rival of the transposes** came in one of twelve profiles. In the others the clock stays at 1.00 from the eight transposes (999.36 in after) to the barrier. In no_keep it fell at 1008.2, 7.4 us behind them, and the way to the barrier took 1.5 us more, near the 1.4 that the rival was priced at. That the transposes did it isn't shown; no run takes them away. The Trainium skill, page TensorE: Matmul & The Clock Gate, Part 4: PE-mode transpose, says that a transpose doesn't count as busy in the way a matmul does; here eight clock-keeping rows, all output matmuls and the mixing stand around them, so the case neither bears it out nor speaks against it.
- **The mixture's start, 5.9 forecast.** 5.35 at the barrier, as read. The other 0.5 is in steps 0 to 9, together with about 0.5 of pace and the router's wait: 0.86 in the pair. In seven of nine profiles a cost stands against it that no part of the prediction has: the clock falls in the third widening, 1.5 us. The step that failed is "what is late next?": I asked it of operands only. The change puts the small jobs of four tiles in one row (32 router matmuls and 8 transposes, 4.3 us) where 16 and 8 stood, 2.6 us.
- **The widening, 3.8 forecast.** 2.52 over 52 steps is 3.1 over 64. Taking the middle between 0.230 and 0.235 was the choice; both paces are there, each in its steps: 0.231 where weights and rows lie in one region, 0.234 where the weights lie in w_q's space and the rows don't.
- **The new wait, 0.6 forecast.** 0.23 at widening 8 and 0.2 at the end (narrowing 62 starts at 1296.38, 0.34 after the last row before it, where 0.12 is the distance without a wait). The place of the first is six steps earlier than I had it: the router's chain on ACT and DVE causes it, not the held additions. The slower rival's cover of 4.2 is confirmed: 3.9 us of chain (chain_2, by the same 0.48 a copy) cost nothing in steady steps, 4.36 cost 0.33 a pair. Its turning point is not: by the prediction the change becomes slower from a chain of 4.64 on, and at 4.36 it was already 7 us slower than before. I had put the price at the excess over the cover, 0.14 here; to this come 0.1 for the slow start behind a wait, and the first ten and the last steps, which lost 7.6 us together.

What stays open: the first turn of the cross attention (up to 1.4 us), whether the new stage one shortens the second sublayer, what gives back 0.8 us within stage one, and how the medians' 12.0 to 13.5 us divide among all this.

## What to carry to other kernels

When a change regroups small jobs on PE, look at what then stands in a row: here matmuls of 8 columns kept the engine busy without a gap, and in most profiles the clock was down for the next large ones. Read a term's base in two or three profiles before you subtract from it, above all where it ends on a transfer, and read a gain where the stage ends, not at the first step that comes earlier. And when operands are doubled in width, half as many steps also means half the cover for every chain that runs beside PE: work out the chain, and test it by making it longer.

## What the runs showed of the hardware

- 512-column matmuls with a new weight each took 0.231 us from start to start with both operands in one region of SBUF and 0.234 with weights in w_q's space and rows elsewhere (a widening's time over twelve); a third buffer moved eighteen widenings from 2.81 to 2.77 and six from 2.78 to 2.80. With 256 columns the same layout gave 2.87, 2.84 and 2.80 for a widening, the old one 2.84 throughout. What in the addresses decides it isn't shown.
- In seven of nine profiles the clock fell to 1.2 GHz for 3.4 us (the stretch of slow rows, 1023.0 to 1026.4 in after_again) behind 32 matmuls of 8 columns and 8 transposes, though PE had no gap; in the mixture's start never behind 16 and 8 (five profiles). When the row of 32 was moved, the fall began inside it and lasted 6.8 us (one profile).
- In before_again twelve rows of the projection take 2.77 us, those of 1.2 GHz, while the window shows a granted clock of 1.00. In before the first twelve take 2.44, also under a granted clock of 1.00. Rows of equal work are the safer witness at the start of a trace.
- DVE's product of two 128x1024 tiles took 1.23 us in both profiles before and 2.08 to 2.10 beside POOL's subtractions of 128x512 in eleven of the twelve profiles of changed kernels (1.75 in combined).
